# Own key tile of the probs x values product: three terms of the first two query groups in shared contraction rows

## The reference, cut to what matters

```python
q = (x @ Wq); k = (x @ Wk); v = (x @ Wv)      # heads of 128
scores = einsum(q, k) * scale, masked causally
probs = softmax(scores)
out = einsum('bhqk,bhkd->bhqd', probs, v)
return out @ Wo
```

## Time and profile before

| | |
|---|---|
| median of 3 runs | 675.08 us (674.37 to 675.57) |
| span of the profiled execution | 673.6 us |
| TensorE busy | 657.9 us, 98% of the span, 3605 matmuls |
| VectorE busy | 531.2 us, 79% |
| ScalarE busy | 416.8 us, 62% |
| GpSimd busy | 259.1 us, 38% |
| DMA | 71.80 MB, mean 107 GB/s |

### The profile page before, as it was taken

How to read it: one execution, slowest core, us unless ns; L and a number is a source line. 1 busy time by engine, 2 the same in 40 slices (tenths; PEclk the granted TensorE clock), 3 DMA queues, 4 the chain that set the end, 5 groups by cost and what they waited for, 6 DMA issues and landing times.

```text
span 673.6 us, 11403 instructions
## 1 busy us (share of the span) xinstructions
PE 657.9 (98%) x3605; PEld 340.6 (51%) x3605; DVE 531.2 (79%) x1728; ACT 416.8 (62%) x1081; POOL 259.1 (38%) x246
## 2 busy tenths in 40 slices
PE   7899999999999999999999999999999999999996
PEld 3455455455555555455555545455554545455553
DVE  3899778867897688867797688867788578789866
ACT  3796665666556765667566765667556667866331
POOL 1686870166013750166013650167003613352231
PEclk9999999999999999999999999999999999999999
DMA  9357375354914285244924285353835247252602
GB/s 300 139 125 158 74 176 110 65 78 84 239 37 94 49 187 110 54 89 78 231 52 93 48 177 114 49 101 69 201 54 100 49 79 173 56 103 46 111 18 93
DMA packets 200779, 71.80 MB, mean 107 GB/s; under 512 B 169744, under 2 KB 192784, under 8 KB 200720
## 3 DMA queue, kind: packets, MB, share of 16 engines
q1 hardware_dynamic: 199376, 70.04, 48.4%
q10 hardware_dynamic: 1344, 1.05, 0.6%
HBM read 27.02 MB, written 2.10 MB: 43 GB/s over the span
## 4 chain that ended last, share of the span: by engine, by line
PE 89%; DVE 5%; DMA 3%; ACT 1%; POOL 1%; issue 1%; SPq 0%; DVEq 0%; POOLq 0%
PE bank L1259 23%; PE bank L1210 21%; PE bank L1249 15%; PE bank L1234 12%; PE bank L1222 5%; PE bank L1190 4%; PE bank L1291 2%; PE bank L1203 2%; PE bank L1193 2%; DMA pT<-p 2%; DVE p L1065 1%; PE bank L1183 1%; DVE pr L1045 1%; DVE rowmax L946 1%; PE bank L1302 1%
## 5 line engine op out<-in xcount | busy, mean ns | idle before, releaser
L741 POOL TENSOR_SCALAR raw<-raw,scale_of 128x512 f32<-128x512 f32 (+1 forms) x75 | 120.6, 1608 | 315.3 <-ACT wk L807 189.1
L1045 DVE CUSTOM_DVE_ANT_0 pr<-bank,mask,back_of 128x32 f32<-128x32 f32 (+15 forms) x256 | 125.3, 496 | 58.4 <-PE bank L1234 57.6
L863 ACT ACTIVATE pr<-pr,mx 128x288 f32<-128x288 f32 (+15 forms) x256 | 131.0, 512 | 61.2 <-DVE mx L1045 60.3
L1210 PE MATMUL bank<-xT,wq 128*128 128x512 f16 x720 | 164.5, 379 | 0.3 <-DVE y L1082 0.3
L872 ACT ACTIVATE p<-pr,ri 128x32 f16<-128x32 f32 (+15 forms) x256 | 118.4, 511 | 49.7 <-DVE ri L1056 49.5
L1065 DVE SCALAR_TENSOR_TENSOR p<-pr,ri,p 128x448 f16<-128x448 f32 (+15 forms) x256 | 128.4, 545 | 15.9 <-ACT p L872 14.7
L1234 PE MATMUL bank<-kT,qT 128*128 128x32 f16 (+15 forms) x768 | 122.2, 279 | 3.9 <-DVE qT L925 2.4
L1249 PE MATMUL bank<-pT,v 128*128 128x512 f16 x480 | 122.8, 379 | 0.8 <-DMA pT<-p 0.7
L1210 PEld LDWEIGHTS bank<-xT,wq 128*128 128x128 f16 x720 | 70.2, 98 | 82.1 <-DVE y L1082 0.8
L1234 PEld LDWEIGHTS bank<-kT,qT 128*128 128x128 f16 x768 | 67.7, 98 | 62.4 <-issue 3.9
L1259 PE MATMUL bank<-wo_odd,oT 128*128 128x512 f16 x384 | 96.1, 379 | 0.0
(11 more groups left out here) (145 smaller groups left out, 692.3 us busy)
## 6 DMA issues: line engine op xcount, KB each, us to landing
raw<-in_wo SPq DMA_DIRECT2D x32, 256.0 KB, 3.5
raw<-in_wq SPq DMA_DIRECT2D x30, 256.0 KB, 3.9
raw<-in_wk SPq DMA_DIRECT2D x8, 256.0 KB, 4.3
raw<-in_wv SPq DMA_DIRECT2D x8, 256.0 KB, 4.1
y<-in_x SPq DMA_DIRECT2D x1, 2048.0 KB, 13.0
pT<-p SPq DMA_TRANSPOSE x128, 3.7
out<-y SPq DMA_DIRECT2D x8, 256.0 KB, 2.0
pT<-in_xT SPq DMA_DIRECT2D x6, 256.0 KB, 7.7
```

Of the source, the lines that this page charges most:

```text
L741: eng.tensor_scalar(whole, raw_of(name, key), scale[0], None, ALU.mult).then_inc(sems["scaled"], 1)
L863: eng.activation(pr[:, t % 2, h, 0:w], pr[:, t % 2, h, 0:w], ACT.Exp, bias=mx[:, k:k + 1], scale=-1.0, accum_out=rs[:, k:k + 1]).then_inc( ...
L1045: eng.tensor_tensor_reduce(out=pr[:, t % 2, h, 0:w], in0=psum("S", t, h)[:, 0:w], in1=mask[:, 0:w], scale=score_scale(t), scalar=BIG, op0= ...
L1210: made = eng.matmul(out, wq[:, g % 2, w, h, c * 128:(c + 1) * 128], xT[:, x, c, b * 512:(b + 1) * 512], start=c == 0 and w + x == 0, stop= ...
```

## The change

In the own key tile only, and for the first two groups of queries.

Group 0 has 32 keys in the own tile, and 4 x 32 = 128 contraction rows are there. Its three terms are put in one matmul: p's part 1 now holds, as own tile, 32 zeros, the 32 low halves, and the 32 high halves twice; a new tile of values, vx (part 0), holds in the matching rows zeros, the values' high halves, their low halves and their high halves. Group 1 has 64 keys: p's part 2 holds the 64 high halves twice, vx (part 1) the values' low halves and their high halves; the low x high term stays a matmul of its own. Groups 2 and 3 have their three terms as before, now as 256 columns. So the own tile's product goes from three matmuls of 512 columns to three of 256 and three of 128. The other key tiles keep three matmuls of 512.

The order of parts in p becomes low of group 2q, high of 2q, high of 2q + 1, low of 2q + 1. ScalarE writes the second copy of the high halves (one more instruction each for groups 0 and 1 where the step has further key tiles; a repeated read where i = 0). VectorE writes group 0's low halves of the own tile in an instruction of its own. The transpose of pair 0 leaves out its first 128 columns. The zeros are written by other fills. vx is filled by five DMAs from v16 for each (p, b), 40 in all, issued by SP after it has seen the low halves of all four value tiles of that (p, b); 32 of its rows are zeroed once by GpSimd. PV of the own tile waits for all five. The list `evicted` puts the five, one at a time, behind a "rest" or "fetch" step that follows the fourth Vp_lo, and those that are left in front of the PV or "rest" that needs them. The program is built with `dynamic_dma_scratch_size=1024`.

```diff
     if name == "PV":
         u = key[0] // NI
-        return [("Vp_lo", u // B // 2, 4 * (u % B) + key[1])]
+        packed = [("VX", u // B // 2, u % B, n) for n in range(VX_PARTS)] if key[1] == key[0] % NI else []
+        return [("Vp_lo", u // B // 2, 4 * (u % B) + key[1])] + packed
+    if name == "rest" and key[0] > 1:
+        u = (key[0] - 2) // NI
+        return [("VX", u // B // 2, u % B, n) for n in range(VX_PARTS)]
...
+            if ready[p, b] == 4:
+                waiting.extend(("VX", p, b, n) for n in range(VX_PARTS))
...
+        for x in [x for x in waiting if x in needed]:
+            waiting.remove(x)
+            yield x
         held = [x for x in held if x not in needed and x != (name, *key)]
         yield (name, *key)
+        packed((name, *key))
+        if name in ("rest", "fetch") and waiting:
+            yield waiting.pop(0)
...
+        vx = sb("vx", [128, 2, NV, 256], f16)
...
                     eng.dma_start_transpose(
-                        pT16[:, 2 * (t % 2) + q, 0:cols].rearrange("p (c n) -> p c n", n=128),
-                        probs(t, q)).then_inc(sems[f"turned{q}{t % 2}"], 16)
+                        pT16[:, 2 * (t % 2) + q, c0:4 * w].rearrange("p (c n) -> p c n", n=128),
+                        p16[:, at + c0:at + 4 * w]).then_inc(sems[f"turned{q}{t % 2}"], 16)
+                elif name == "VX":
+
+                    p, b, n = key
+                    s = v_slot(p, 4 * b)
+                    for tt in range(4 * b, 4 * b + 4):
+                        sp_.wait_ge(*done("v_lo", p, tt))
+                    to, part, of, at = ((0, 1, 1, 64), (64, 1, 0, 64), (32, 0, 0, 96), (64, 0, 1, 96), (96, 0, 0, 96))[n]
+                    eng.dma_start(vx[to:to + 128 - at, part, s:s + 4, :], v16[at:128, of, s:s + 4, :]).then_inc(sems[f"vx{p}{b}"], 16)
...
+                    eng.memset(vx[0:32, 0, :, :], 0.0).then_inc(sems["vx_zero"], 1)
...
-                    for m in range(2 - q):
-                        made = eng.memset(both[:, :, m, 0:96 - 32 * (2 * q + m)], 0.0)
+                    for part, n in ((0, 32), (1, 32)) if q else ((1, 32), (3, 64)):
+                        made = eng.memset(own_part(t, q, part)[:, 0:n], 0.0)
...
-                        eng.activation(halves_of_probs(t, h)[0], pr[:, t % 2, h, 0:group(t, h)[1]], ACT.Copy,
+                        w, n = group(t, h)[1], 32 * (h + 1)
+                        if q == 0 and w == n:
+
+                            twice = pr[:, t % 2, h, 0:n].rearrange("p (a n) -> p a n", a=1).to_broadcast([128, 2, n])
+                            eng.activation(own_part(t, 0, h + 1)[:, 128 - 2 * n:128].rearrange("p (a n) -> p a n", a=2), twice, ACT.Copy,
+                                           scale=ri[:, 1, k:k + 1]).then_inc(sems["p_hi"], 1)
+                            continue
+                        if q == 0:
+                            eng.activation(own_part(t, 0, h + 1)[:, 128 - 2 * n:128 - n], pr[:, t % 2, h, 0:n], ACT.Copy, scale=ri[:, 1, k:k + 1])
+                        eng.activation(halves_of_probs(t, h)[0], pr[:, t % 2, h, 0:w], ACT.Copy,
                                        scale=ri[:, 1, k:k + 1]).then_inc(sems["p_hi"], 1)
...
-                        made = eng.scalar_tensor_tensor(out=lo, in0=pr[:, t % 2, h, 0:group(t, h)[1]], scalar=ri[:, 1, k:k + 1], in1=hi,
-                                                        op0=ALU.mult, op1=ALU.subtract)
+                        w, n = group(t, h)[1], 0
+                        if h == 0:
+
+                            n = 32
+                            made = eng.scalar_tensor_tensor(out=own_part(t, 0, 1)[:, 32:64], in0=pr[:, t % 2, h, 0:n], scalar=ri[:, 1, k:k + 1],
+                                                            in1=hi[:, 0:n], op0=ALU.mult, op1=ALU.subtract)
+                        if n < w:
+                            made = eng.scalar_tensor_tensor(out=lo[:, n:w], in0=pr[:, t % 2, h, n:w], scalar=ri[:, 1, k:k + 1], in1=hi[:, n:w],
+                                                            op0=ALU.mult, op1=ALU.subtract)
...
-                    for a, p in half3:
-                        made = eng.matmul(out, v16[:, a, s, cols], turned_of(t, j, p).rearrange('p a m (h n) -> p a m h n', n=32), start=j == 0 and a + p == 0,
-                                          stop=j == i and a == 1)
-                    if j == i:
-                        made.then_inc(sems["PV"], 1)
+                    turned = turned_of(t, j)
+                    hi, lo = turned[:, :, 1:3, :], turned[:, :, 0:4:3, :]
+                    vh, vl = v16[:, 0, s, cols], v16[:, 1, s, cols]
+                    if j < i:
+                        for v, p in ((vh, hi), (vh, lo), (vl, hi)):
+                            eng.matmul(out, v, p.rearrange("p a m (h n) -> p a m h n", n=32), start=j == 0 and v is vh and p is hi, stop=False)
+                    else:
+
+                        pe.wait_ge(*done(f"vx{g // 2}{b}", VX_PARTS - 1))
+                        pe.wait_ge(*done("vx_zero"))
+                        late = out[:, 1, :, :, :]
+                        eng.matmul(late, vh, hi[:, 1, :, :].rearrange("p m (h n) -> p m h n", n=32), start=j == 0, stop=False)
+                        eng.matmul(late, vh, lo[:, 1, :, :].rearrange("p m (h n) -> p m h n", n=32), start=False, stop=False)
+                        eng.matmul(out[:, 0, 1, :, :], vh, lo[:, 0, 1, :].rearrange("p (h n) -> p h n", n=32), start=False, stop=False)
+                        eng.matmul(late, vl, hi[:, 1, :, :].rearrange("p m (h n) -> p m h n", n=32), start=False, stop=False)
+                        eng.matmul(out[:, 0, 1, :, :], vx[:, 1, s, cols], hi[:, 0, 1, :].rearrange("p (h n) -> p h n", n=32), start=False, stop=False)
+                        eng.matmul(out[:, 0, 0, :, :], vx[:, 0, s, cols], hi[:, 0, 0, :].rearrange("p (h n) -> p h n", n=32), start=False,
+                                   stop=True).then_inc(sems["PV"], 1)
...
-    nc = bacc.Bacc("TRN2", target_bir_lowering=False, num_devices=1)
+    nc = bacc.Bacc("TRN2", target_bir_lowering=False, num_devices=1, dynamic_dma_scratch_size=1024)
```

More of the change, by code:

```diff
@@ L10 @@
 NV = 16
+VX_PARTS = 5
 TWO15 = 32768.0
@@ L34, in reads, with packed @@
         u = key[0] // NI
-        return [("Vp_lo", u // B // 2, 4 * (u % B) + key[1])]
+        packed = [("VX", u // B // 2, u % B, n) for n in range(VX_PARTS)] if key[1] == key[0] % NI else []
[3 more added lines that the diff above has]
+        return [("VX", u // B // 2, u % B, n) for n in range(VX_PARTS)]
     return [("O_lo", key[0])] if name == "W" else []
 def evicted(steps):
-    held, given = [], set()
+    held, given, ready, waiting = [], set(), {}, []
+    def packed(step):
+        if step[0] == "Vp_lo":
+            p, b = step[1], step[2] // 4
+            ready[p, b] = ready.get((p, b), 0) + 1
+            if ready[p, b] == 4:
+                waiting.extend(("VX", p, b, n) for n in range(VX_PARTS))
     for name, *key in steps:
@@ L50, in evicted @@
             yield x
+            packed(x)
+        for x in [x for x in waiting if x in needed]:
+            waiting.remove(x)
+            yield x
         held = [x for x in held if x not in needed and x != (name, *key)]
         yield (name, *key)
+        packed((name, *key))
+        if name in ("rest", "fetch") and waiting:
+            yield waiting.pop(0)
         if name == "S":
@@ L395, in post_ln_block @@
             "ht": ["ht", "hwT_hi", "hwT_lo"],
-            "consts": ["mask0", "ident0", "ident", "ident16_0", "ident16", "mhalf", "ones8", "ik", "mask"],
+            "consts": ["mask0", "ident0", "ident", "ident16_0", "ident16", "mhalf", "ones8", "ik", "mask", "vx_zero"],
             "bias": ["bb64_hi", "bb64_lo", "ones_r"],
@@ L458, in post_ln_block @@
                 count(f"turned{key[1]}{key[0] % 2}", key[0], by=16)
+            elif name == "VX":
+                count(f"vx{key[0]}{key[1]}", key[2], by=16)
             elif name == "PV":
@@ L599, in group, with own_part, turned_of @@
             return 15 - (4 * (t % NI) + b), 32 * (4 * (t % NI) + b + 1)
[L601 to L605, removed]
+        def own_part(t, q, part):
+            w = 128 * (t % NI + 1)
+            at = 4 * w * (t % NI + q) + part * w
+            return p16[:, at:at + 128]
         def halves_of_probs(t, b):
-            both = probs(t, b // 2).rearrange("p (s m n) -> p s m n", s=2, m=2)
-            return [both[:, s, b % 2, 96 - 32 * b:] for s in range(2)]
-        def turned_of(t, j, s):
+            w = 128 * (t % NI + 1)
+            at = 4 * w * (t % NI + b // 2)
+            return [p16[:, at + part * w + 96 - 32 * b:at + (part + 1) * w] for part in ((1, 0) if b % 2 == 0 else (2, 3))]
+        def turned_of(t, j):
             w = 128 * (t % NI + 1)
             two = 2 * (t % 2)
-            x = pT16[:, two:two + 2, 0:4 * w].rearrange("p a (s h n) -> p a s h n", s=2, h=2)
             c = t % NI - j
```

(6 more changed lines are left out.)

2 lines of the change are left out of this document (1 added, 1 removed).

## The result

The changed kernel takes 705.93 us (705.28 to 707.6, 4 runs), the kernel before 675.17 us (674.37 to 675.57, 4 runs): a ratio of 1.0465, 95% interval [1.0448, 1.0481], which is 31.4 us slower by the ratio and 30.8 by the medians. Forecast were 689.7 us and a range of 677 to 700. Direction and place were right, the size was not.

What follows compares the result with a forecast made beforehand. TensorE's columns, in a fixed order of steps, were taken as the bound. Saving -9.2, waits +19.1, softmax path +2.0 and clock +2.7 gave +14.6 us on 675.08, so 689.7 us; range 677 to 700 us.

Steps and rivals of the forecast that it cites:

- The saving of 9.8 us: Own key tile on TensorE: 651 ns of matmuls become 498 ns, 153 ns saved in each of 64 tiles.
- The rival that they would not stream: Own tile's narrow matmuls: each 128-column one costs up to 110 ns for 56, 10.4 us more, 700 us; chance 3%.
- the extra copies: ScalarE's second copies of high halves: at most 31 us of busy time on an engine idle for a third, not the bound.
- The 2.0 us put down for the softmax path: Pair 0's transpose issued up to 0.6 + 0.2 us later: between zero and 8 us, taken as 2 us.
- the four steps: PV at t = 4, 20, 36, 52 waits for b = 1 packing: 5.4, 4.5, 5.1, 4.1 us, sum 19.1 us.
- the DMAs ahead of VX4: On SP, VX4, the fifth packing DMA, goes behind rest(21,1), VX3 and a fetch at t = 20, landing at 242.4.
- what TensorE gains or loses ahead of it: At t = 4 the wait hangs on GpSimd, so tiles 0 to 3's saving and a PV(0, 0) wait don't count.
- b = 0, p > 0: ... Nothing.: Places of these packing DMAs: the fifth is issued over 100 steps before its PV needs it, so no cost.
- Their volume I cost at nothing: The 40 packing DMAs move 3.7 MB while DMA engines stand idle half of the steady part: no cost.
- I count one, 2.7 us.: TensorE's clock falling at the long waits: between none and four falls, 0 to 10.8 us, one counted at 2.7 us.
- four falls: Rival: the waits occur and the clock falls at three or four of them, 695 to 698 us; chance 15%.
- The rival on the other side: Packing lands in time, no waits at t = 4, 20, 36, 52: 666 to 667 us; chance 11%.

Runs made afterwards that it cites:

- mended version: e1_early with the (0, 0) packing again one DMA at a time and PV(0, 0) one Q product later: 668.08 us, 0.9903 of the kernel before.
- e4_no_copies: e1_early without ScalarE's second copies of the high halves in steps t of 4 and later: 671.31 us, 0.9946 of the kernel before.
- e9_b0_spread: Mended version with all b = 0 packing one DMA at a time behind rest and fetch steps, b = 1 at once: 673.39 us, ratio 0.9982.
- e10_b1_spread: Mended version with the four b = 1 packing sets spread as in the changed kernel: 699.16 us, 1.0357 of the kernel before.
- e7_early_unused: Kernel before plus the packing DMAs, issued at once and waited for, with vx unused and products unchanged: 677.47 us, ratio 1.0042.
- e6_filler_full: Changed kernel with 96, 98 and 78 throwaway matmuls before the vx waits at t = 20, 36, 52: 700.14 us, 1.0389 of the kernel before.
- e1_early: Changed kernel with all five packing DMAs of a (p, b) issued at once behind the fourth Vp_lo: 670.34 us, 0.9933 of the kernel before.
- e2_filler: Changed kernel with 36 to 75 throwaway matmuls before the vx waits at t = 0, 4, 20, 36, 52: 705.22 us, ratio 1.0439.
- e3_waits_alone: Kernel before plus the packing DMAs in the changed kernel's places and TensorE's wait, vx unused, products unchanged: 708.14 us, ratio 1.0481.

## Why the prediction was right or wrong

**What bounds the kernel, and the products.** Right. The own tile's matmuls of 256 and 128 columns came 109 and 56 ns apart (median of 64 of each line, in the changed kernel's trace and in the mended version's). The saving of 9.8 us is there as 9.2 us less of busy time in the mended version. The rival that they would not stream is refuted. The Trainium skill, "TensorE: Matmul & The Clock Gate", section "Back-to-back issue gap", gives about 81 ns for sustained pairs of load and 128-column matmul. This trace does not agree: it has 56 ns.

**ScalarE, VectorE, GpSimd.** Right in kind: the extra copies cost nothing measurable at the end (e4_no_copies), the fill of vx took 3.5 us in GpSimd's idle time. The 2.0 us put down for the softmax path were not found there; the pT waits of about that size came from SP's queue (e9_b0_spread, e10_b1_spread).

**The place of the packing.** Right, and the main result: the forecast named the four steps, the DMAs ahead of VX4 and nearly the size. Waits forecast at 5.4, 4.5, 5.1 and 4.1 us were 5.96, 5.45, 5.60 and 4.39, in sum 21.4 for 19.1. A packing's issue on SP took 0.51 to 0.59 us in these steps, not 0.45, and the copy at t = 20 released TensorE 2.8 us after its issue, not 2.5. Spreading b = 1 alone again costs the mended version 30.6 of the 31.4 + 6.5 = 37.9 us that lie between it and the changed kernel.

**Steps that failed.**
- *"... what TensorE gains or loses ahead of it, the own tiles 0 to 3 and a possible wait at PV(0, 0) for the first VX4, does not reach the end."* PV(0, 0) waited 2.79 us for its packing and the clock fell behind it. The fetch that I took as pinned by GpSimd at 88.11 went out at 91.21: GpSimd's piece had moved with the rest, and TensorE was let go at 94.53, not 91.0. What looked like a fixed time hangs on the same chain: at 85.60 GpSimd had waited 1.25 us for ScalarE's half of a piece of wo.

```profile
90.04 1.15 POOL L780 TENSOR_TENSOR wo_odd<-raw,wo_odd 128x512 f16<-128x512 f32 x1
...
91.21 0.34 SPq L698 DMA_DIRECT2D raw<-in_wo  x1
```

- *"b = 0, p > 0: ... Nothing."* and *"Their volume I cost at nothing"*. For the volume it holds (e7_early_unused). For the places of b = 0 it does not: 5.3 us (e9_b0_spread). I had asked only who waits for these copies, not what is queued behind them on SP.
- *"I count one, 2.7 us."* The largest miss, and the step that put the time out of the range. All four long waits and the one in the opening brought a fall, and a sixth came without a wait for vx. In the changed kernel's trace the clock fell 2.1, 3.5, 4.7 and 3.4 us into the long waits and each time stayed down for 6.8 us, so 3.0 to 6.0 us of it lay behind the wait. The matmuls slowed down cost 12.9 us by the busy time, in place of 2.7. Net of what is lost again to later landings, the three steady falls are worth 5 us (e6_filler_full). The rows I had the earlier trace rows gave one idle stretch at the end, in which the clock stayed up for some 4 us, and one cold start, and I took one fall of four for no better reason than that; four falls were a rival with 15%, whose 698 us was still short for want of the other two steps. The price of a fall was read from a stretch in which the granted clock reads 1.00 (5 to 11 us), so that no row showed it to be one. That 2.7 us came near what a long wait's fall took in slower matmuls, 1.5 to 3.0 us, is luck: the number of falls failed, six for one.

In sum, the profile is 30.9 us longer where 14.6 were forecast, 16.3 us more. By its busy and idle times 5.1 of them are waits for vx (24.2 for 19.1: 2.8 in the opening, 2.3 in the four long waits), 10.2 slower matmuls (12.9 for 2.7) and 1.6 the other waits (3.6 for 2.0), less 0.6 for the saving of the first four tiles, which I had given up. What each of these is worth at the end is another question, and the 5 us of e6_filler_full and the 5.3 us of e9_b0_spread show that it is not the same number.

**The rival on the other side** (packing in time, 666 to 667 us) is what the mended version nearly is, at 668.1. It was a question of the order of one list, not of whether the idea works.

## What to carry to other kernels

When work is added to an in-order queue, follow the list and ask two things of each item: what stands ahead of it when its reader arrives, and what is queued behind it; both cost here, 30.6 and 5.3 us. Data that a full TensorE will wait for is to be issued as soon as its source is ready, even at the price of a block of issues, with an exception for the opening, where the queue is itself late. And a wait of 4 to 6 us on a kernel that is bound by TensorE cost more than its length here, as the clock fell in it: keeping it up through three such waits gave back 1.7 us for each.

## What was not expected of the hardware

The clock was lost with every one of TensorE's whole waits for vx of 3.9 to 6.0 us in these runs, and also with shorter ones: 2.79 us in the opening of the changed kernel, 2.99 us in that of e1_early, and in e2_filler 3.28 us behind 75 small matmuls and 2.12 us at 72.86 us. But a wait of the same length at the same PV(0, 0) kept it in two other runs, 2.87 us in e3_waits_alone and 2.77 us in e6_filler_full, where the clock read 1.00 from 52 to 56 us:

```profile
52.48 0.27 PE L1313 MATMUL bank<-pT,v 128*128 128x256 f16 x1 [2.77 <-DMA vx<-v]
```

So its length alone does not tell what such a wait costs. Nor was the time at half clock always 6.8 us: behind the 5.87 us wait at t = 4 in e6_filler_full it was 3.4. In the changed kernel's trace it also fell in the opening, at 29.2 us, where TensorE had waited 1.66, 0.28 and 0.52 us shortly before; the kernel before has the same three waits there and kept its clock, and so did the mended version. Which of the two happens was not controlled by any of the edits. That fall cost next to nothing: the changed kernel was 0.70 us ahead of the kernel before at its wait of 1.66 us and still 0.57 us at 46.2, as slower matmuls took the place of short waits there.

A copy of 64 or 128 KB within SBUF landed 2.3 to 2.4 us (median) from its issue, as the changed kernel's DMA issues show, no sooner than a 256 KB store:

```profile
vx<-v SPq DMA_DIRECT2D x16, 128.0 KB, 2.3
out<-y SPq DMA_DIRECT2D x8, 256.0 KB, 2.1
...
vx<-v SPq DMA_DIRECT2D x24, 64.0 KB, 2.4
```
